# Attention and experts on one core: turned rows and router placed one batch later, projections and output one gap later

## The reference

```
q, k, v = x @ Wq.T, x @ Wk.T, x @ Wv.T          # 16 heads, 16 features, 64 values
k_enc, v_enc = x[:, :128] @ Wk_enc.T, x[:, :128] @ Wv_enc.T
taylor_exp(x) = [1, x/2, outer(x, x)/sqrt(2)/4]
A_qk  = tril(taylor_exp(q) . taylor_exp(k))      # causal
A_qk2 = taylor_exp(q) . taylor_exp(k_enc)        # not masked
z   = 1 / (sum of the weights of a query + 1e-12)
out = (A_qk @ v + A_qk2 @ v_enc) * z
x   = layernorm(x + out @ Wout.T)
logits = x @ wr + br                             # then softmax, top 2, gate, expert top1
x   = layernorm(x + gate * expert(x))
```

## Time and profile before

| | |
|---|---|
| median of 3 runs | 1182.94 us (1181.48 to 1186.81) |
| the profiled execution | 1180.28 us |
| its span | 1178.5 us |
| TensorE matmul, busy | 1063.4 us (90%) |
| VectorE, busy | 634.1 us (54%) |
| GpSimd, busy | 613.0 us (52%) |
| ScalarE, busy | 508.0 us (43%) |
| SP's queue, share of 16 DMA engines | 31.5% |

### The profile page before, as it was taken

One profiled execution on the slowest core, in us unless ns is written; L12 is line 12 of the kernel. 1 busy time (PEld: TensorE's weight loads), 2 busy tenths in 40 slices (PEclk: granted clock), 3 DMA queues, 4 the chain that ended last, 5 costly groups with the idle time before them and its releaser, 6 DMA issues. The chain is left out here.

```text
span 1178.5 us, 16833 instructions
## 1 busy us (share of the span) xinstructions
PE 1063.4 (90%) x5296; PEld 621.4 (53%) x5297; DVE 634.1 (54%) x963; ACT 508.0 (43%) x891; POOL 613.0 (52%) x635
## 2 busy tenths in 40 slices
PE   5699899989989989989999998883679999999994
PEld 4344355445445445436545544463357766766763
DVE  5396864683693683585476468447123343333332
ACT  2466644654654663653664464400123233233231
POOL 1397654664673674665576567500134544444442
PEclk9799989999999999999999998995789999999998
DMA  5733631741651552453273261104821011101010
GB/s 208 260 102 106 201 125 64 234 151 41 201 178 69 176 176 97 141 181 126 70 217 122 84 208 59 36 1 197 349 116 33 29 31 34 33 29 33 30 30 1
DMA packets 54111, 134.91 MB, mean 114 GB/s; under 512 B 5854, under 2 KB 10176, under 8 KB 51746
## 3 DMA queue, kind: packets, MB, share of 16 engines
q1 hardware_dynamic: 50306, 124.81, 31.5%
q0 software_dynamic: 3744, 9.31, 2.5%
HBM read 87.73 MB, written 47.29 MB: 115 GB/s over the span
## 5 line engine op out<-in xcount | busy, mean ns | idle before, releaser
L384 ACT ACTIVATE w<-slot 128x1024 f32<-128x1024 f32 (+1 forms) x256 | 231.2, 916 | 176.3 <-PE slot L730 176.1
L751 PE MATMUL osum<-w,values 128*64 128x512 f32 (+3 forms) x1280 | 253.6, 492 | 5.7 <-DVE w L511 5.7
L508 DVE SCALAR_TENSOR_TENSOR w<-w,mask 128x256 f32<-128x256 f32 (+1 forms) x192 | 175.8, 916 | 150.8 <-ACT w L384 138.0
L343 POOL TENSOR_TENSOR wsum<-w 128x512 f32<-128x512 f32 x64 | 95.7, 1496 | 222.7 <-DVE w L511 222.7
L511 DVE TENSOR_SCALAR w<-w 128x768 f32<-128x768 f32 (+2 forms) x192 | 189.4, 986 | 0.0
L347 POOL TENSOR_TENSOR wsum<-wsum,w 128x768 f32<-128x768 f32 x64 | 124.8, 1951 | 60.0 <-DVE w L511 58.2
L1161 ACT ACTIVATE active<-upT,b 128x128 f32<-128x128 f32 x312 | 84.9, 383 | 158.3 <-PE upT L1239 158.3
L1215 PE MATMUL down<-w,active 128*128 x624 | 144.1, 385 | 2.5 <-ACT active L1161 2.5
L1227 PE MATMUL up<-w,rowsT 128*128 x312 | 143.1, 602 | 0.7 <-ACT rowsT L1150 0.7
L730 PE MATMUL slot<-qop,kop 64*128 64x512 f32 (+3 forms) x640 | 126.6, 426 | 9.8 <-issue 7.2
L1215 PEld LDWEIGHTS down<-w,active 128*128 128x128 f32 x624 | 117.5, 193 | 18.6 <-issue 3.8
(11 more groups left out here) (187 smaller groups left out, 1210.7 us busy)
## 6 DMA issues: line engine op xcount, KB each, us to landing
kop<-k_rows SPq DMA_DIRECT2D x32, 640.0 KB, 5.8
qop<-q_rows SPq DMA_DIRECT2D x32, 512.0 KB, 7.5
w<-in_w SPq DMA_DIRECT2D x16, 1024.0 KB, 9.3
inv<-inv_rows SPq DMA_DIRECT2D x56, 256.0 KB, 4.5
k_rows<-kh SPq DMA_DIRECT2D x32, 320.0 KB
k_rows<-kl SPq DMA_DIRECT2D x32, 320.0 KB
q_rows<-qh SPq DMA_DIRECT2D x32, 256.0 KB
q_rows<-ql SPq DMA_DIRECT2D x32, 256.0 KB
```

The source lines that it names most:

```text
L343: pool.tensor_tensor(dst[:, 0, :], src[:, 0, 0:N], src[:, 0, N:2 * N], ALU.add)
L384: act.activation(w[:, n % 2, :, at:at + cols], slot[u % 2][:, :, 0:cols], ACT.Square, bias=HALF_ROOT).then_inc(squared, 1)
L508: dve.scalar_tensor_tensor(src[:, :, 0:cut], src[:, :, 0:cut], 0.5, mask[:, 0:cut].unsqueeze(1).to_broadcast([P, 2, cut]), ALU.add, ALU.mu ...
L751: last = pe.matmul(osum[n % 2][HD * s:HD * s + HD, q0:N], values[:, j, h * HD:h * HD + HD], w[:, n % 2, s, at:at + N - q0], start=(u == 0) ...
```

## The change

The rows of a batch are no longer turned and routed in gaps 26, 28 and 30 of the batch that follows it. They are turned in gaps 7 and 9 and routed in gap 10 of the batch after that one; only the last batch still does those of the batch before it in 26, 28 and 30, and so it has both. The blocks of query and key projections go from gaps 10, 12, 14, 25, 27 to 11, 13, 15, 27, 29, those of the output from 15, 17, 19, 21 to 16, 18, 20, 22, the early value blocks one gap later, one late value block from gap 5 to 4. Moments, reciprocal deviation and centring go one gap later, one normalisation from 12 to 11. The ring `att` has 13 places instead of 14. `load_rows` for the batch before is issued after the inverses, and waits as ever for the transposes that read `y`.

```
-RING, ATT, INV = 4, 14, 4
-V_LATE_AT = {0: 0, 1: 1, 3: 2, 5: 3, 6: 4}
-QK_AT = {10: 0, 12: 1, 14: 2, 25: 3, 27: 4}
-OUT_AT = {15: 0, 17: 1, 19: 2, 21: 3}
-V_EARLY_AT = {16: 0, 18: 1, 20: 2, 22: 3, 24: 4}
-TURN_AT, ROUTER_AT = {26: 0, 28: 1}, 30
+RING, ATT, INV = 4, 13, 4
+V_LATE_AT = {0: 0, 1: 1, 3: 2, 4: 3, 6: 4}
+QK_AT = {11: 0, 13: 1, 15: 2, 27: 3, 29: 4}
+OUT_AT = {16: 0, 18: 1, 20: 2, 22: 3}
+V_EARLY_AT = {17: 0, 19: 1, 21: 2, 23: 3, 25: 4}
 XH_GAP, XL_GAP = 7, 8
-NORM_AT = {4: 0, 5: 1, 6: 2, 7: 3, 9: 4, 10: 5, 12: 6, 13: 7}
-INVERT_GAP, MOMENTS_GAP, CENTRE_GAP, RSTD_GAP = 1, 22, 24, 23
+NORM_AT = {4: 0, 5: 1, 6: 2, 7: 3, 9: 4, 10: 5, 11: 6, 13: 7}
+INVERT_GAP, MOMENTS_GAP, CENTRE_GAP, RSTD_GAP = 1, 23, 25, 24
...
+def turned_at(b, g):
+
+    if b >= 2 and g in (7, 9, 10):
+        return [(b - 2,) + {7: ("turn", 0), 9: ("turn", 1), 10: ("router", 0)}[g]]
+    if b == B - 1 and g in (26, 28, 30):
+        return [(b - 1,) + {26: ("turn", 0), 28: ("turn", 1), 30: ("router", 0)}[g]]
+    return []
...
@@ sync
                     for g in range(2, PAIRS // 2):
                         load_inverse(b - 1, g)
+                if b > 1:
+                    load_rows(b - 1)
                 gather(b, 3)
...
-                if b > 0:
-                    load_rows(b)
+            load_rows(B - 1)
...
@@ tensor (scalar and vector, one gap later, in the same way)
-                    if b > 0 and g in TURN_AT:
-                        turn_rows(b - 1, TURN_AT[g])
-                    if b > 0 and g == ROUTER_AT:
-                        router(b - 1)
+                    for owner, kind, k in turned_at(b, g):
+                        if kind == "turn":
+                            turn_rows(owner, k)
+                        else:
+                            router(owner)
```

More of the change, by code:

```diff
@@ L63, in piece_numbers @@
                 order.append((b + 1, "v", V_EARLY_AT[g]))
[L64 to L67, removed]
+            order += turned_at(b, g)
     order += [(B - 1, "turn", k) for k in range(2)] + [(B - 1, "router", 0)]
@@ L456, in _ @@
                         copy_values(b + 1, 0, V_EARLY_AT[g - 1])
-                    if b > 0 and g - 1 in TURN_AT:
-                        copy_turned(b - 1, TURN_AT[g - 1])
+                    for owner, kind, k in turned_at(b, g - 1):
+                        if kind == "turn":
+                            copy_turned(owner, k)
                     if b + 1 < B and g == XH_GAP:
@@ L594, in _ @@
                         residual(b - 1, OUT_AT[g - 1])
-                    if b > 0 and g - 1 == ROUTER_AT:
-                        logits_of(b - 1)
+                    for owner, kind, _ in turned_at(b, g - 1):
+                        if kind == "router":
+                            logits_of(owner)
                     if n < B * PAIRS and u > 0:
```

## The result

The changed kernel takes 1215.59 us (median; 1214.08 to 1216.93), the kernel before beside it on the same chip 1182.21 (1180.29 to 1186.81). The ratio is 1.0276, with an interval of [1.0244, 1.0309]: slower by 33.4 us, twice what I forecast (+16.6) and outside my range. The profiled execution has a span of 1213.6 us against 1178.5.

A forecast was written before the change was run, and what follows sets the result against it. VectorE was taken to bound the front and TensorE the tail; -18.6 + 2.8 + 20 + 3 + 2.9 + 7.5 - 1 = +16.6 on the median 1182.94 gave 1199.5 us, range 1177 to 1214.

The forecast's parts named there:

- The tail: From first output block to next gap 0, TensorE-bound: 3.1 us less in each of six batches, -18.6.
- The front: From first normalisation to first output block, VectorE-bound: first output at A+31.1, a loss of 2.8 us for five batches.
- A: The moment in each batch when VectorE starts normalising, after its wait for the inverses; 418.39 in batch 4.
- the front loses 31.1 - 26.0 - 4.55 = 0.55 per batch: First output block moves from A+26.0 to A+31.1, less 4.55 us of added TensorE work: 2.8 for five batches.
- The bounds of the step, -1.75 and +1: Range for the front's 0.55 us loss per batch; the better end, -1.75, has VectorE never idle.
- A itself moves: q is sent later, so the inverses load later: A 4.0 us later (3.1 to 5.1), five times, 20.
- Batch 7: Last batch: only the operands are in the way, without `xT`; 3 us taken (0 to 4).
- Clock: Longer TensorE wait before the first projection, lower granted clock: 1.5 us for each of five fronts, 7.5 (0 to 15).
- Other edits at 0: Value block, `att` ring of 13, `load_rows`, moments and centring one gap later: each claimed to cost 0.
- The wait for `qop` "costs nothing": At gap 4 TensorE waits some 1 to 3 us for `qop`, at no cost, since A is later still.
- The rule of the queue: DMA descriptors are consumed in ring order, the small inverse store sitting behind large transfers; by it the sum is +16.6.
- The second rival: Faster: load of the inverses follows its own store as transfers ahead drain sooner, A stays: -16.8, 1166.1 us, chance 0.16.

The follow-up runs named there:

- the kernel with q sent at 14.1: Kernel before with rows turned in gaps 7, 8, routed in 9, fourth and fifth projections in 23, 25, rows' store behind second send: 1168.0 us, ratio 0.9896.

## Why the prediction was wrong in size

The direction and the mechanism held; the sum did not, since one saving stands in it twice. By its steps:

- **The tail**: predicted 47.7 from first output block to gap 0, measured 47.67 to 47.81. Right.
- **The front**: first projection at A+16.6 predicted, 16.54 to 16.59 measured; VectorE idle 2.7 against 2.99; first output block at A+31.1 against 30.7 to 31.2. Right to 0.4. The run with the router one gap earlier confirms that it hangs on where VectorE reads the router's bank.
- **The step that failed is "the front loses 31.1 - 26.0 - 4.55 = 0.55 per batch"**, as a term beside "6 x -3.1 = -18.6". On these numbers the front becomes longer by 5.1. Of the 4.55 subtracted from that, 1.48 is the gap that the tail gave to the front, and belongs there. The other 3.1 is the tail's saving, and it stood in the -18.6 already. It was counted twice, for five batches: 15.5. Without it the same steps give 16.6 + 15.5 = +32.1, 1215.0 us for the kernel that measured 1215.59. By the measured durations of the table: +4.9 in the front, -4.5 in the tail, so moving the rows earned nothing in batches 2 to 6, where I had booked 3.1 less 0.55 for each. The bounds of the step, -1.75 and +1, carry the same error (and the working in them gives -2.0, not -1.75).
- **A itself moves**: predicted by 4.0 (3.1 to 5.1), measured 5.3. q left 6.7 before gap 0, as forecast. From there to the load took 20.98 to 22.95, mean 22.2 where I took 21.7; I had measured from batch 5's load at 10.95, where the mean of the five batches was 10.5; and the load took 0.2 longer. Over five batches that is 6.5 more than forecast. Batch 1: 2.9 forecast, 2.9 measured. Batch 7: 3 forecast, 3.5 measured.
- **Clock**: 7.5 (0 to 15) forecast, and no cost to be seen: the fronts came at the 31.1 that had been worked out from durations without it. TensorE's wait before the first projection, forecast at 5.5, was 2.05 to 5.36. The granted clock did fall, to 0.83 to 0.89 in the five fronts against 0.87 to 1.00 before. Batches 3 and 5, and the middle of batch 3's front:

```profile
335.67:366.41 30.74, 25.44 (x148) 12.44 (x146) 27.47 (x31) 16.26 (x22) 21.69 (x14) 0.83 0.52 168
533.81:564.51 30.70, 24.47 (x148) 12.30 (x147) 27.49 (x31) 16.27 (x22) 21.70 (x14) 0.89 0.53 170
...
350.00:355.00 5.00, 2.79 (x6) 1.82 (x6) 5.00 (x7) 0.00 (x0) 4.33 (x4) 0.50 0.66 246
```

  0.83 and 0.89 give the same length. The low clock fell where TensorE was busy for 2.79 of 5.00 us and VectorE for all of them, so it was hidden, unlike in batch 3 of the kernel with the router one gap earlier. That this miss, 7.5, and the previous one, 6.5, cancel is luck. Batch 0, forecast 1 shorter, was 0.4 shorter.
- **Batch 7** also has a front longer by 1.9, its tail and end 0.9, for which I had no term. The gap of the output block and the rows of batch 5 lie in that front now.
- **Other edits at 0**: the table above leaves nothing for the value block, the ring of 13 or `load_rows`, and the kernel with the rows alone, which has them all, equals the kernel before. That fits 0; none of them was run by itself. The centring at 0 was right as long as q was late for another reason, and cost some 14 once that was removed.
- **The wait for `qop` "costs nothing"**: it came, 1.7 to 3.5 in each of seven batches, and A was later still in all of them. That it is hidden follows from the order of the rows (TensorE resumes at 428.18, A is at 435.16). I did not take it away alone.
- **The rule of the queue**: the load went out 0.8 after `xT` landed in the changed kernel too, and 0.8 after `qop` when `xT` was moved away. The forecast built on it held. The second rival lost with its condition, that the transfers ahead drain sooner; the kernel with q sent at 14.1 met that condition and gained.

What stays open: in the changed kernel I can't tell how the 5.0 of the front divides between the router's bank and the tables moved by one gap, beyond the fact that the router one gap earlier gave back 1.8 to 3.2 in four of five batches. And why the granted clock stayed low to the end of the front of batch 3 in that kernel and not in its neighbours is not shown by these traces.

## What to carry to other kernels

Add up a change along one cut of the time axis: the length of each stretch after, minus its length before, and nothing else. A saving that is written as a term of its own and again as "added work that was paid for" is the easiest error to make and the hardest to see, since every single duration is right. Before moving the last producer of a batch, list everything that must be issued after it on its queue, and count back from the point where the result is needed: here 22 us of transfers lay between the send of q and the load of the inverses, so taking work out from between them moves the wait and does not shorten the batch. When undoing an edit changes nothing, look in the issuing engine's program for what stands directly ahead: two waits may have moved together.

## What the runs showed of the hardware that I had not expected

- A transfer of 32 KB that took 2.4 us to its successor's issue on an idle queue took 5.8 on an otherwise empty queue of another engine while two transfers of 512 KB were under way. A queue of their own let the store and its load go some 2 us earlier, and the load's longer flight (7.5 to 9.6 against 4.8 to 5.6, to A) took them back with interest.
- A dependent DMA issued by ScalarE held up what stood behind it in ScalarE's program, by 6.08 in batch 3: 3.6 for the wait and 2.4 for the issue of four loads.
- What a low granted clock cost depended on where it lay: at 0.50 for 5 us in which TensorE was busy for 2.79, the front took the same 30.7 as one at 0.89 on average; at 0.50 for 9.4 us in which TensorE had no gap, a front took 5.5 more than its neighbour with the same program.
